# Layer 0's attention: the second query tile's scores from rounded parts, and w_lo made earlier on GpSimd

## What is computed

```python
q = rmsnorm(x @ Wq_a, q_norm_w) @ Wq_b          # 16 heads of 128 + 64 columns
kv = rmsnorm(x @ Wkv_a, kv_norm_w) @ Wkv_b
k_rot, q_rot = apply_rope(x @ Wk_rope), apply_rope(q_rot)
scores = einsum('bqhd,bkhd->bhqk', qf, kf) * 192 ** -0.5
p = softmax(where(causal, scores, min))
o = einsum('bhqk,bkhd->bqhd', p, v).reshape(B, T, H * 128) @ Wo
```

## Time and profile before

| | us |
|---|---|
| time, median of 3 runs | 534.26 (533.25 to 538.05) |
| the profiled execution's own time | 533.59 |
| its span, first to last instruction | 531.1 |
| TensorE busy | 497.8 (94%) |
| VectorE busy | 380.4 (72%) |
| ScalarE busy | 339.7 (64%) |
| GpSimd busy | 294.0 (55%) |

### The profile page before, as it was taken

One profiled execution on the slowest core, in us unless ns is written; L12 is line 12 of the kernel. 1 busy time (PEld: TensorE's weight loads), 2 busy tenths in 40 slices (PEclk: granted clock), 3 DMA queues, 4 the chain that ended last, 5 costly groups with the idle time before them and its releaser, 6 DMA issues.

```text
span 531.1 us, 10729 instructions
## 1 busy us (share of the span) xinstructions
PE 497.8 (94%) x3592; PEld 434.7 (82%) x3592; DVE 380.4 (72%) x833; ACT 339.7 (64%) x761; POOL 294.0 (55%) x289
## 2 busy tenths in 40 slices
PE   8999999999999996899958979999999999999994
PEld 7668888888888785688836869999999999999883
DVE  4798888888883275655537897779857985588556
ACT  5756777777766646344324776778766876676663
POOL 5757677767764136255551676776554664465330
PEclk9999999999999999899987988999999999999998
DMA  8939999940000672455564000000000000000001
GB/s 270 398 85 383 314 331 318 322 151 0 0 1 1 225 295 81 114 156 162 181 216 171 0 1 2 1 0 2 1 2 1 1 2 0 2 1 1 0 22 60
DMA packets 17756, 56.78 MB, mean 107 GB/s; under 512 B 2628, under 2 KB 12362, under 8 KB 15914
## 3 DMA queue, kind: packets, MB, share of 16 engines
q1 hardware_dynamic: 14960, 49.81, 27.5%
q0 software_dynamic: 2752, 6.40, 3.6%
HBM read 49.19 MB, written 28.45 MB: 146 GB/s over the span
## 4 chain that ended last, share of the span: by engine, by line
PE 78%; DVE 7%; ACT 5%; issue 3%; DMA 3%; POOL 2%; SPq 0%; DVEq 0%; POOLq 0%; ACTq 0%
PE bank L443 10%; PE bank L445 10%; PE bank L444 10%; PE bank L991 5%; PE bank L586 5%; PE bank L508 4%; PE bank L611 3%; PE bank L1008 3%; PE bank L588 2%; PE bank L735 2%; PE bank L720 2%; PE bank L722 2%; PE bank L721 2%; PE bank L622 2%; PE bank L702 2%
## 5 line engine op out<-in xcount | busy, mean ns | idle before, releaser
L1100 ACT ACTIVATE probs<-bank,neg_max,q_scale 128x256 f32<-128x256 f32 (+1 forms) x128 | 63.7, 507 | 39.1 <-DVE neg_max L1770 39.1
L1986 POOL TENSOR_TENSOR probs<-probs,inv_sum 128x512 f32<-128x512 f32 x64 | 51.5, 826 | 44.1 <-DVE inv_sum L1778 44.1
L2019 POOL TENSOR_TENSOR exps<-exps,tables 128x256 f32<-128x256 f32 x32 | 24.7, 771 | 75.2 <-ACT exps L1210 75.0
L1210 ACT ACTIVATE exps<-bank 128x768 f32<-128x768 f32 x32 | 25.9, 808 | 41.3 <-PE bank L702 41.3
L1590 DVE TENSOR_TENSOR q_lo<-q_sum,q_hi 128x512 fp32r<-128x512 f32 x32 | 28.8, 899 | 29.0 <-ACT q_hi L1164 28.6
L2006 POOL TENSOR_TENSOR swapped<-swapped,tables 128x512 f32<-128x512 f32 x32 | 43.4, 1359 | 5.2 <-ACT swapped L1131 5.1
L2115 POOL DMA_INDIRECT y_rows<-y_slot,dest x31 | 29.7, 959 | 30.0 <-issue 18.2
L1756 DVE TENSOR_TENSOR swapped<-bank,tables 32x512 f32<-32x512 f32 x64 | 44.4, 693 | 1.4
L1978 POOL TENSOR_TENSOR qT<-qT,swapped 128x512 f32<-128x512 f32 x32 | 40.8, 1274 | 6.1 <-DVE swapped L1756 6.1
L443 PE MATMUL bank<-x,wq_hi 128*128 128x256 f32 x128 | 38.6, 301 | 0.1
L586 PE MATMUL bank<-keysT,qT 128*128 128x256 f32 x128 | 38.2, 380 | 0.0
(11 more groups left out here) (281 smaller groups left out, 1766.6 us busy)
## 6 DMA issues: line engine op xcount, KB each, us to landing
slots<-in_c_unused SPq DMA_DIRECT2D x20, 1036.0 KB, 35.5
gu_all<-in_gate_up SPq DMA_DIRECT2D x4, 1024.0 KB, 7.8
xg<-slots SPq DMA_DIRECT2D x31, 129.5 KB, 2.2
wvo_raw<-in_wvo SPq DMA_DIRECT2D x1, 2560.0 KB, 18.4
dn_all<-in_down SPq DMA_DIRECT2D x1, 2048.0 KB, 7.7
wq_full<-in_Wq SPq DMA_DIRECT2D x1, 2048.0 KB, 17.8
wo_raw<-in_Wo SPq DMA_DIRECT2D x1, 2048.0 KB
wqk_raw<-in_wqk SPq DMA_DIRECT2D x1, 1536.0 KB, 9.9
```

Source lines behind the costliest of these rows:

```text
L1100: ins = act.activation(probs[:, par, h, c0:c1], bank[:, 2 * par + h, c0:c1], ACT.Exp, bias=neg_max[:, par, i:i + 1], scale=q_scale[:, b, t ...
L1986: ins = pool.tensor_tensor(some, some, inv, ALU.mult)
```

## The change

In units 4 to 31 the scores of the second query tile are no longer two fp32 products but six of rounded parts (three for each head). For that the operands are split. The keys are split once: ScalarE makes the high parts in units 1 and 2 behind the exps, GpSimd the low parts behind its normalise. The second query tile of unit n+2 is split in unit n: ScalarE copies it into `q_parts` behind the exps (`act_second_hi`), GpSimd subtracts behind its normalise (`pool_second_lo`). The scores then wait for q_lo as well. GpSimd makes w_lo of pair p+2 at the end of pair p's last unit, ahead of the rope sum of that unit; before, it made it at the start of the next unit, behind that rope sum. Because of the `p + 2 < PAIRS` in that rule, pairs 5 and 6 are taken out of the loop and stand as straight code. keysT keeps two of its four planes, the raw queries of the setup get a buffer of their own, and some semaphores are merged under one name with other counts.

```diff
+        q_parts = sb("q_parts", [P, 2, B, 2, P], F32R, second)
...
-    keysT = sb("keysT", [P, G, B * T])
+    keysT = sb("keysT", [P, 2, B * T])
+    with ExitStack() as first:
+        q_raw_all = sb("q_raw_all", [P, NT * QL], F32, first)
+    keysT_parts = sb("keysT_parts", [P, 2, B * T], F32R)
...
-        with eng.Fori(0, PAIRS // 2 - 1) as two:
+        with eng.Fori(0, PAIRS // 2 - 2) as two:
             pair(2 * two + 1, 1, False, True)
             pair(2 * two + 2, 0, False, True)
+        pair(PAIRS - 3, 1, False, True)
+        pair(PAIRS - 2, 0, False, True)
         pair(PAIRS - 1, 1, False, False)
...
                 eng.wait_ge(at["q_ready"], n + 1)
+                if not (isinstance(p, int) and p == 0):
+                    eng.wait_ge(at["q_lo"], n - 3)
+                    if isinstance(n, int) and n == 4:
+                        eng.wait_ge(su["key_steps"], 6)
...
-                    eng.matmul(dst[:, 0:T], q[:, P:T], keysT[:, 0, T * b:T * b + T],
-                               start=True, stop=False, skip_group_check=True)
+                    keys = slice(T * b, T * b + T)
+                    if isinstance(p, int) and p == 0:
+                        eng.matmul(dst[:, 0:T], q[:, P:T], keysT[:, 0, keys], start=True, stop=False,
+                                   skip_group_check=True)
+                    else:
+                        three_pass(eng, dst[:, 0:T], q_parts[:, 0, b, h, :], q_parts[:, 1, b, h, :],
+                                   keysT_parts[:, 0, keys], keysT_parts[:, 1, keys], True, False)
...
+    def second(p, b, more):
+
+        if b < 2:
+            return None if isinstance(p, int) and p == 0 else (p, b + 2)
+        return (p + 1, b - 2) if more else None
+
+    def second_tile(p, b):
+        return qT[:, :, T * b + P:T * b + T]
+
+    def act_second_hi(act, at, p, b):
+
+        act.wait_ge(at["q_ready"], 4 * p + b + 1)
+        act.activation(q_parts[:, 0, b, :, :], second_tile(p, b), ACT.Copy).then_inc(at["q_hi"], 1)
+
+    def pool_second_lo(pool, at, p, b):
+
+        m = 4 * p + b
+        pool.wait_ge(at["q_ready"], m + 1)
+        pool.wait_ge(at["q_hi"], m - 3)
+        pool.tensor_tensor(q_parts[:, 1, b, :, :], second_tile(p, b), raw(q_parts[:, 0, b, :, :]),
+                           ALU.subtract).then_inc(at["q_lo"], 1)
...
                 ins.then_inc(at["exp_done"], 1)
+                if isinstance(n, int) and 1 <= n < 3:
+                    some = slice(512 * n - 512, 512 * n)
+                    act.activation(keysT_parts[:, 0, some], keysT[:, 0, some], ACT.Copy).then_inc(su["keysT_copied"], 1)
+                if second(p, b, more):
+                    act_second_hi(act, at, *second(p, b, more))
...
-            if b == 0 and more:
-                split_w_low(pool, at, p + 1, 1 - odd)
+            if isinstance(n, int) and n == 0:
+                split_w_low(pool, at, 1, 1)
             if own:
                 pool_normalise(pool, at, n, b % 2)
+            if isinstance(n, int) and 1 <= n < 3:
+                some = slice(512 * n - 512, 512 * n)
+                pool.wait_ge(su["keysT_copied"], n + 2)
+                pool.tensor_tensor(keysT_parts[:, 1, some], keysT[:, 0, some], raw(keysT_parts[:, 0, some]),
+                                   ALU.subtract).then_inc(su["key_steps"], 1)
+            if own and second(p, b, more):
+                pool_second_lo(pool, at, *second(p, b, more))
+            if own and b == B - 1 and (not isinstance(p, int) or p + 2 < PAIRS):
+                split_w_low(pool, at, p + 2, odd)
             if own and ahead(p, b, more):
                 pool_sin(pool, at, *ahead(p, b, more))
```

More of the change, by code:

```diff
@@ L149, in build @@
     q_minus = sb("q_minus", [P, B, 2])
+    with ExitStack() as second:
+        q_parts = sb("q_parts", [P, 2, B, 2, P], F32R, second)
     with ExitStack() as blocks:
@@ L261, in build @@
     key_raw = qT[:, 1, :].rearrange("p (t f) -> p t f", f=P)
-    q_raw = keysT[:, 2:4, :].rearrange("p g n -> p (g n)")[:, 0:NT * QL].rearrange("p (t n) -> p t n", n=QL)
+    q_raw = q_raw_all[:].rearrange("p (t n) -> p t n", n=QL)
     key_sq = q_sum[:, 0, :].rearrange("p (t n) -> p t n", n=KVL)
@@ L306, in build @@
               "k_hi k_lo v_done v_copied ones")
-    ff = sems("ffn", "abs_done halved bwT_done bw_hi bw_lo")
-    at0 = sems("a0", "w_hi_done w_lo_done q_done cos_done sin_done q_ready scores_done exp_done inv_ready ctx_done "
+    ff = sems("ffn", "act_steps halved bwT_done bw_lo")
+    at0 = sems("a0", "q_hi q_lo w_hi_done w_lo_done q_done cos_done sin_done q_ready scores_done exp_done inv_ready ctx_done "
                "ctx_copied max_step max_ready probs_ready probsT_done probsT_copied")
@@ L473, in pe_logits @@
         if b == 0:
-            eng.wait_ge(mo["region_ready"], 1)
+            eng.wait_ge(mo["ids_ready"], 2)
         else:
@@ L1257, in act_layer1 @@
                 act.activation(fw_hi[:], bank[:, MORE, :].rearrange("p (k o) -> p k o", k=KD),
[L1258 removed]
+                               ACT.Copy).then_inc(ff["act_steps"], 1)
             if n == 2 * PAIRS + 1:
@@ L1357, in _ @@
         act.wait_ge(su["fold_q_copied"], 4)
-        act.wait_ge(su["q_scaled"], 2)
+        act.wait_ge(su["rms_var"], 4)
         act_attention0(act, at0)
@@ L1391, in step @@
             dve.wait_ge(dve_step, counted(ins))
-        dve.wait_ge(ff["abs_done"], 2)
+        dve.wait_ge(ff["act_steps"], 2)
         step(dve.tensor_scalar(square_sum[:, 1, 0:2], square_sum[:, 0, 0:2], 1.0 / D, None, ALU.mult))
@@ L1687, in dve_layer1 @@
             if n == 2 * PAIRS:
-                dve.wait_ge(ff["bw_hi"], 1)
+                dve.wait_ge(ff["act_steps"], 3)
                 dve.tensor_tensor(fw_lo[:], bank[:, MORE, :].rearrange("p (k o) -> p k o", k=KD), raw(fw_hi[:]),
@@ L1846, in _ @@
         inv = inv_dev[:, 0, :].rearrange("p (b t) -> p b t", t=2)
-        dve.tensor_scalar(q_scale[:], inv, scale, None, ALU.mult).then_inc(su["q_scaled"], 1)
-        dve.tensor_scalar(q_minus[:], inv, -scale, None, ALU.mult).then_inc(su["q_scaled"], 1)
+        dve.tensor_scalar(q_scale[:], inv, scale, None, ALU.mult).then_inc(su["rms_var"], 1)
+        dve.tensor_scalar(q_minus[:], inv, -scale, None, ALU.mult).then_inc(su["rms_var"], 1)
         dve.wait_ge(ld["tables_in"], 16)
         dve.wait_ge(su["key_steps"], 3)
-        dve.wait_ge(su["q_scaled"], 2)
+        dve.wait_ge(su["rms_var"], 4)
         dve_cos(dve, at0, 0, 0)
@@ L1902, in _ @@
         dve.wait_ge(ld["route_in"], 16)
-        dve.tensor_copy(x_rows[:, :, D + 2], row_ids).then_inc(mo["row_ids"], 1)
-        dve.tensor_copy(region_bf[:], region_at).then_inc(mo["region_ready"], 1)
+        dve.tensor_copy(x_rows[:, :, D + 2], row_ids).then_inc(mo["ids_ready"], 1)
+        dve.tensor_copy(region_bf[:], region_at).then_inc(mo["ids_ready"], 1)
         step(dve.memset(eps, LN_EPS))
@@ L2104, in _ @@
         pool.wait_ge(ld["unused_in"], 16 * REGIONS)
-        pool.wait_ge(mo["row_ids"], 1)
+        pool.wait_ge(mo["ids_ready"], 1)
         for b in range(B):
```

6 lines of the change are left out of this document (3 added, 3 removed).

## The result

The changed kernel takes 532.5 us (median of 18 runs, 530.17 to 534.72) against 534.35 us for the kernel before (18 runs, 532.59 to 538.69): ratio 0.9958, 95% interval 0.9937 to 0.9978. A repetition of the same two kernels later gave 533.44 against 534.78, ratio 0.9975 (0.9952 to 0.9998). So it is faster by 1.3 to 2.2 us by the two ratios. I had put it at 530.4. That is 3.9 under the first median of 534.26, of which 3.4 are the sum and the rest comes from starting near the profiled execution's 533.59; a third to somewhat more than half of the 3.9 came. "Within 1%", the likeliest of the three outcomes, was right.

A forecast was written before the change was run, and what follows sets the result against it. TensorE was taken to bound layer 0's attention, at 4.32 us a unit plus a lock wait of 0.23 in four units. Gains of 3.4 from the profiled 533.59 gave 530.2, put at 530.4; range 528.4 to 534.3.

The forecast's parts named there:

- the sum: Layer 0's attention: 0.25 us gained in units 4 to 7, 2.5 in 8 to 27, 0.65 in 28 to 31, together 3.4.
- TensorE's saving: Second-tile scores: three rounded products for one fp32 save 0.08 us a head, 0.16 a unit; TensorE's unit falls to 4.16.
- The subtraction: GpSimd's added 128x256 subtraction, between normalise and rope sum in 28 units: 0.73 us, 0.69 from start to start.
- Case B: Rival: the lock stops mattering because GpSimd's subtraction costs 0.61 us or less; four units 16.7, time 528.6; chance 0.18.
- The lock: VectorE's neg_max multiply, two SBUF inputs, waits for GpSimd's current instruction; it now meets the subtraction, at most 0.73 us.
- Case D: Rival: GpSimd keeps the lock from one instruction to the next; four units 18.0 us, time 537; chance 0.07.
- case E: Rival: rounded products with operands from ScalarE and GpSimd take 0.145 us each, nothing saved; time 533.6 to 535; chance 0.03.
- GpSimd's line: GpSimd's normalise, subtraction and rope sum take 3.49 us of a 4.16 unit; w_lo makes it 4.72 in every fourth unit.
- The walk: Carried unit to unit, normalise distances of 4.72, 3.5, 4.07 and 4.73 us; four units take 17.0 against 17.51.
- The start: First units of the stage: GpSimd's added splits delay the subtraction for unit 4 to 48.55, against 47.97 wanted; 0.6 us lost.
- The step that failed: ScalarE's added copy, taken as 0.3 us and hidden; the probsT copy comes 0.3 later and TensorE waits for it nowhere.
- Case C: Rival: GpSimd becomes the bound behind w_lo, TensorE waits 0.6 us or more; gain 0 to 1, time 533.2; chance 0.22.

The follow-up runs named there:

- e2: The changed kernel with ScalarE's copy of the second query tile moved behind its copies of probsT and the context; 530.0 us, ratio 0.9895 to the kernel before.
- e8: The kernel of e7 with keysT split in the setup instead of in units 1 and 2; 528.2 us, ratio 0.9873 to the kernel before.
- e6: The kernel before with the row maxima in PSUM, so that neg_max has only one input in SBUF; ratio 0.9989 to the kernel before.
- e7: The kernel of e2 with the row maxima in PSUM, as in e6; ratio 0.9872 to the kernel before.
- e5: The changed kernel without the query splits after unit 4's: later rounded scores reuse those parts, w_lo stays ahead of the rope sum; ratio 0.991 to the kernel before.

## Why the prediction was right, and where it failed

- **TensorE's saving** was right: 4.17 a unit (predicted 4.16), which leaves no room for a cost of the switch between kinds of product.
- **The subtraction** was right: 0.73 in all 28. Case B, which needed 0.61, falls. By the figure for each element in the Trainium skill (GPSIMD Engine Reference, Elementwise — side-by-side cycle accounting) my estimate was 0.55, and the measurement decides against it.
- **The lock** was right: L1813 takes at most 0.72 (predicted 0.73), so it never waits for two GpSimd instructions in a row, and the waits for L1756 are gone. Case D falls by this, and case E by the 4.17 a unit.
- **GpSimd's line** was right: 4.75 behind w_lo in e2 (predicted 4.72). **The walk** gave the four lengths of e2 to 0.03 and their sum, but not all of its way there. Its o is the time from a normalise to the next neg_max. In the unit with w_lo, neg_max arrives at o = 1.18 in e2 (103.42 against the normalise of 102.24), where the walk had 1.01; by its rule that would leave TensorE a wait of 0.22, and the trace has 0.4. The next values of o are 0.59 and 1.62, where the walk had 0.45 and about 1.5. So the bound of 1.57 is passed one unit sooner and the distance of 4.74 comes ahead of the 4.04. That the sum still came out at 17.0 is in part luck. In the changed kernel itself they are 4.73, 3.74, 4.73 and 4.04, and only the second is off, because the exps behind the late copies start at 110.16, 0.30 after L1813 has ended.
- **The start** cost the predicted 0.6 (e8 took it back: the first group fell from 17.39 to 16.79).
- **The step that failed** is the one on ScalarE's copy: "The probsT copy comes 0.3 later too; TensorE waits for it nowhere in this stage". I moved probsT by the copy's duration alone. The copy also waits for the rope sum, and the same change puts w_lo, 1.24 from start to start, in front of that. In one unit of four probsT came 1.3 late (1.00 of wait and 0.32 of copy). I had written of w_lo that "Queued behind it are the rope sum, needed two units later, and the next normalise": the rope sum was then needed at once, by an instruction that the change itself had added. The price is 5.2 us of TensorE's weight loads in 7 units, some 0.74 each. It takes the place of the 0.38 for the normalise, which no longer shows as a wait, so it adds about 0.4 in four units: 17.4 on average instead of 17.0.
- Over the stage: units 8 to 27 gained 0.65 instead of 2.5, units 0 to 7 lost 0.20 where 0.25 were to come, and the last four gained 0.30 instead of 0.65, 0.75 in all. Case C had the right size (a gain of 0 to 1 in the stage) for another reason: it put the wait on the normalise.
- The time came out within the range and nearer to the forecast than the stage did. That is luck: 0.4 of the time's gain lies outside all instructions, and nothing in the prediction had it.

## What to carry to other kernels

A short instruction added to an engine that works in program order can cost its own wait too, and everything behind it pays: ask of each added instruction when its last input is ready after the change, not before it, and place it behind the work for which the bound engine waits. An instruction that "is needed two units later" stops being so when the change adds an early reader. And a stage of 145 us that repeats to 0.1 us in the trace tells far more than a time that moves by 0.8 when a kernel is compared with itself. Take care where such a stage is cut, though: a mark that a lock can delay makes single groups of units look faster or slower than they are.

## What the runs showed of the hardware

- VectorE's 128x4 multiply with both inputs in SBUF took 0.16 to 1.26 us, by which GpSimd instruction it met; with one input in PSUM, 0.161 to 0.164 in each of its 96 runs in e6, e7 and e8.
- Work added to GpSimd can shorten that wait: with a 0.73 us subtraction at the place where a 1.27 us sum stood, the longest was 0.72 (changed kernel, e2) and not 1.26 (e5).
- GpSimd's subtraction of 128x256 with a rounded output took 0.722 to 0.742, and 0.68 from start to start; ScalarE's copy of the same size took 0.42, and 0.30 to 0.32 from start to start.
- The time of an execution was 1.76 to 1.86 us above its span in 82 executions of the kernels with the unrolled loop and the added code, and 2.06 to 2.55 in those of the kernels without them.
